# Banded attention with queries and keys in two orders, and one unit of scores per head

## What is computed

```python
OFFSETS = sorted(set(range(0, 33)) | {48, 64, 96, 128, 192, 64, 96, 128, 192, 256, 384})
scores = stack([einsum('bhnd,bhnd->bhn', q, shift(k, delta)) for delta in OFFSETS]) * scale
scores = scores + pos_bias.T[None, :, None, :]          # 16 heads of 16 columns
scores = where(n < delta, -inf, scores)
alpha = softmax(scores, axis=-1)
out = sum over i of alpha[..., i:i+1] * shift(v, OFFSETS[i])
return flat(out) * sigmoid(x @ Wgate + bgate) @ Wout + bout
```

## Time and profile before

| | us |
|---|---|
| median of 3 runs | 3774.55 |
| the profiled execution, its own time | 3782.0 |
| its span, first to last instruction | 3780.3 |
| PE busy in the span | 3176.4 (84%) |
| DVE busy | 1747.6 (46%) |
| ACT busy | 1189.4 (31%) |
| POOL busy | 352.9 (9%) |

### The profile page before, as it was taken

How to read it: one execution, slowest core, us unless ns; L and a number is a source line. 1 busy time by engine, 2 the same in 40 slices (tenths; PEclk the granted TensorE clock), 3 DMA queues, 4 the chain that set the end, 5 groups by cost and what they waited for, 6 DMA issues and landing times. The chain is left out here.

```text
span 3780.3 us, 99336 instructions
## 1 busy us (share of the span) xinstructions
PE 3176.4 (84%) x44860; PEld 1864.3 (49%) x44860; DVE 1747.6 (46%) x3244; ACT 1189.4 (31%) x1486; POOL 352.9 (9%) x334
## 2 busy tenths in 40 slices
PE   1688888888788888879957899999999898997898
PEld 0456565656565666634443444444444444443345
DVE  5334333434333333361074665666666656664302
ACT  0122222222222222232002545554545554553300
POOL 0000000000000000000002111121212121100000
PEclk9788888888788888789957999999999999998896
DMA  5422222222222222126813222222222222312394
GB/s 131 109 68 74 68 74 68 74 71 71 71 71 68 74 68 74 33 92 266 359 15 84 52 52 60 56 56 52 52 53 59 52 60 52 68 19 93 124 419 175
DMA packets 235041, 343.30 MB, mean 91 GB/s; under 512 B 115962, under 2 KB 144452, under 8 KB 218244
## 3 DMA queue, kind: packets, MB, share of 16 engines
q1 hardware_dynamic: 222452, 334.40, 30.9%
q10 hardware_dynamic: 12176, 2.66, 0.5%
HBM read 266.15 MB, written 69.24 MB: 89 GB/s over the span
## 5 line engine op out<-in xcount | busy, mean ns | idle before, releaser
L1351 DVE TENSOR_REDUCE b_tops<-b_slot 128x8 f32<-128x1024 f32 x576 | 680.4, 1220 | 361.5 <-PE b_slot L1208 182.6
L1388 ACT ACTIVATE b_probs<-b_slot 128x1024 f32<-128x1024 f32 x576 | 583.1, 1023 | 551.2 <-PE b_slot L1208 395.5
L711 DVE TENSOR_TENSOR a_probs<-a_scores,a_bias_k 128x512 f32<-128x512 f32 x256 | 176.6, 690 | 554.5 <-PE a_scores L570 318.3
L803 ACT ACTIVATE a_probs<-a_probs 128x512 f32<-128x512 f32 x256 | 161.5, 631 | 589.7 <-DVE a_probs L711 588.6
L1228 PE MATMUL b_outT_ps<-b_probs,b_v 128*17 128x128 f32 (+3 forms) x4608 | 318.0, 384 | 6.2 <-ACT b_probs L1388 5.5
L1208 PE MATMUL b_slot<-b_q_stack,b_k_stack 99*128 99x512 bf16 (+3 forms) x1280 | 275.8, 322 | 43.3 <-DVE b_tops L1351 32.8
L1208 PE MATMUL b_slot<-b_k_stack,b_q_stack 96*128 96x512 bf16 (+3 forms) x1280 | 267.1, 323 | 29.4 <-DVE b_tops L1351 20.6
L1155 POOL TENSOR_SCALAR_AFFINE_SELECT b_probs<-b_probs 128x1024 f32<-128x1024 f32 x128 | 139.8, 1093 | 809.5 <-ACT b_probs L1388 809.5
L1208 PEld LDWEIGHTS b_slot<-b_q_stack,b_k_stack 99*128 99x128 bf16 x1280 | 107.2, 100 | 204.6 <-DVE b_tops L1351 61.9
L1208 PEld LDWEIGHTS b_slot<-b_k_stack,b_q_stack 96*128 96x128 bf16 x1280 | 97.6, 98 | 185.4 <-DVE b_tops L1351 61.6
L1762 PE MATMUL f_ps<-f_w_ring,f_hidT 128*32 128x256 f32 x1024 | 184.0, 381 | 2.1 <-ACT f_hidT L1803 2.1
(11 more groups left out here) (215 smaller groups left out, 4492.1 us busy)
## 6 DMA issues: line engine op xcount, KB each, us to landing
f_w_ring<-in_L_ffn_w_dram SPq DMA_DIRECT2D x128, 1024.0 KB, 10.1
parts_dram<-a_parts SPq DMA_DIRECT2D x96, 256.0 KB
parts_dram<-b_parts SPq DMA_DIRECT2D x96, 256.0 KB
a_k_stack<-parts_dram SPq DMA_DIRECT2D x128, 128.0 KB, 3.0
b_k_stack<-parts_dram SPq DMA_DIRECT2D x64, 256.0 KB, 7.1
a_q_stack<-parts_dram SPq DMA_DIRECT2D x64, 192.0 KB, 3.0
b_q_stack<-parts_dram SPq DMA_DIRECT2D x32, 384.0 KB, 4.6
values_dram<-a_v_stage SPq DMA_DIRECT2D x32, 272.0 KB, 2.6
```

The source lines that it names most:

```text
L711: dve.tensor_tensor(dst[:, :].rearrange("p (t c) -> p t c", c=64), src[:, :].rearrange("p (t c) -> p t c", c=64), bias_k[k][:, HG * g + h, ...
L803: act.activation(dst[:, :], dst[:, :], ACT.Exp).then_inc(probs_ready, 1)
L1351: ins = dve.tensor_reduce(out, src, AX.X, ALU.max)
L1388: act.activation(probs_of(b, g, u, h)[:, :], slot_of(step)[:, :], ACT.Exp).then_inc(taken_act, 1)
```

## The change

- **Two orders.** `parts` holds each part twice, as it is and sorted by residue; the far products read the second copy without a stride (`products`, one function for near and far now). The new step `turn` makes the copies on POOL, three strided copies of 1,024 elements. Spills are three DMAs of 512 KB, a pair's stacks seven DMAs of 1,536 KB in all.
- **Room.** Instead of two sets of stacks of four heads there is a ring of three for two heads each (`ring`). `parts`, `v_near`, `v_far`, `v_stage` and the probabilities have one buffer; the f32 projection `full`, the normalised tokens and `flatT` are one tile.
- **Projections.** q or k is made in one piece of 1,024 columns: DVE adds its bias, ACT rounds `part0`, POOL subtracts (`rest1`), ACT rounds `part1`, POOL subtracts (`part2`) and turns. `part0` waits on ACT until the spill before has landed. They stand in groups 1 (q and k of the first half, both behind the far products) and 3 (q between the scores, k behind the far products).
- **Units.** A unit is one head, near and far together, 128 x 1024: four a group. PSUM is three slots of two banks that scores, maxima and all else share in turn. The next group's maxima of head h follow the scores of head h.
- **Maxima's rows.** `mt` is 16 matmuls into two places (one for each order), taken by DVE and ACT; `mrow` is four DMAs. Both stand ahead of the group's own far products, which now follow its near ones.

The core of the diff:

```diff
-            for step in (which, "part1", "part2"):
-                out += [(step, b, half, c) if step == which else (step, b, half, c, which) for c in range(2)]
-            out.append(("spill", b, half, which))
+            out += [(which, b, half)] + [(step, b, half, which) for step in ("part0", "rest1", "part1", "part2", "turn", "spill")]
...
+            tops = [[("mx",) + after + (h,)] if more else [] for h in range(HG)]
...
+            cuts = [len(first) * k // 3 for k in range(4)]
+            seq += [("vin", b, g), ("S", b, g, 0)] + tops[0] + [("S", b, g, 1)] + operands(n + 3) + tops[1]
+            seq += first[cuts[0]:cuts[1]] + [("S", b, g, 2)] + tops[2] + first[cuts[1]:cuts[2]] + [("S", b, g, 3)] + operands(n + 4)
+            seq += tops[3] + ([("fparts",) + after] if more else []) + first[cuts[2]:cuts[3]] + near[0:4]
+            seq += ([("fp",) + after, ("mred",) + after] if more else []) + near[4:8]
+            seq += ([("mt",) + after, ("mrow",) + after] if more else []) + far
+            seq += last + [("ote", b, g)]
...
+            if g in (1, 3):
+                p = projections(b + 1, g // 2)
+                last = p + last if g == 1 else last
+                first = first + p[0:7] if g == 3 else first
+                last = p[7:] if g == 3 else last
...
+def ring(b, g, pair):
+    return (2 * (b * G + g) + pair) % 3
...
-        parts = [sb(f"parts{m}", [P, PARTS, N], BF16) for m in range(2)]
-        q_stack = [sb(f"q_stack{n}", [ALL_ROWS, HG, N], BF16) for n in range(2)]
-        k_stack = [sb(f"k_stack{n}", [ALL_ROWS, HG, N], BF16) for n in range(2)]
...
+        parts = sb("parts", [P, PARTS, 2, N], BF16)
+        q_stack = [sb(f"q_stack{n}", [ALL_ROWS, 2, 2, N], BF16) for n in range(3)]
+        k_stack = [sb(f"k_stack{n}", [ALL_ROWS, 2, 2, N], BF16) for n in range(3)]
...
+        full = zb[:, :, :].rearrange("p i d -> p (i d)")
...
+        slots = [ctx.enter_context(nc.psum_tensor(f"a_slot{n}", [P, N], F32)) for n in range(3)]
...
-        scores_ps = [ctx.enter_context(nc.psum_tensor(f"a_scores{n}", [P, 512], F32)) for n in range(NS)]
...
-        aux_ps = [ctx.enter_context(nc.psum_tensor(f"a_aux{n}", [P, 512], F32)) for n in range(NA)]
...
+                    elif kind == "rest1":
+                        _, b, half, which = step
+                        pool.wait_ge(part0_done, count("part0", "part0", b, half, which))
+                        pool.tensor_tensor(full, full, parts[:, 0, 0, :], ALU.subtract).then_inc(rest1_done, 1)
+                    elif kind == "part2":
+                        _, b, half, which = step
+                        pool.wait_ge(part1_done, count("part1", "part1", b, half, which))
+                        pool.tensor_tensor(parts[:, 2, 0, :], full, parts[:, 1, 0, :], ALU.subtract).then_inc(part2_done, 1)
+                    elif kind == "turn":
+                        _, b, half, which = step
+                        pool.wait_ge(part2_done, count("part2", "part2", b, half, which))
+                        for part in range(PARTS):
+                            pool.tensor_copy(parts[:, part, 1, :].rearrange("p (r a) -> p r a", r=LINKS),
+                                             parts[:, part, 0, :].rearrange("p (a r) -> p r a", r=LINKS)).then_inc(turned, 1)
...
-                        sp.wait_ge(part2_done, count("part2", "part2", b, half, 1, which))
+                        sp.wait_ge(turned, PARTS * count("turn", "turn", b, half, which))
...
-                            sp.dma_start(scratch["parts"].ap()[m, half, :, part], parts[m][:, part, :]).then_inc(spilled[m], 16)
+                            sp.dma_start(scratch["orders"].ap()[m, half, :, part], parts[:, part, :, :]).then_inc(spilled, 16)
...
+                        sp.wait_ge(spilled, SPILL * count("spill", "spill", b, g // 2, "k"))
+                        if 2 * (b * G + g) + pair >= 3:
+                            b0, g0, pair0 = pair_of(2 * (b * G + g) + pair - 3)
+                            sp.wait_ge(filled, count("filled", "S", b0, g0, 2 * pair0 + 1))
...
+                        for h in range(HG):
+                            sp.dma_start(q_stack[ring(b, g, h // 2)][QK_ROWS:ALL_ROWS, h % 2, :, :], neg_rows[PARTS * h:PARTS * (h + 1), :, :]
+                                         ).then_inc(mrows_in, 16)
...
-                            ins = pe.matmul(dst[RES * r2:RES * (r2 + 1), 64 * pair:64 * (pair + 1)],
-                                            left[rows, h, r:N:LINKS], right[rows, h, r:N:LINKS],
...
+                        ins = pe.matmul(dst[RES * r2:RES * (r2 + 1), at:at + 64], left[rows, h, 1, RES * r:RES * (r + 1)],
+                                        right[rows, h, 1, RES * r:RES * (r + 1)], start=start, stop=True, skip_group_check=True)
...
+                        for at, i in [(at, i) for at in (AT_ROWS, 2 * AT_ROWS) for i in range(NT)]:
+                            ins = pe.matmul(dst[at:at + HG * PARTS, i * P:(i + 1) * P], neg_parts[:, :, :, i].rearrange("p h a -> p (h a)"),
+                                            ident16[:, :], start=True, stop=True, skip_group_check=True)
...
+                        if c == 0 and k == 0:
+                            pe.wait_ge(probs_ready, count("S", "S", b, g, HG - 1))
...
+                    elif kind == "part0":
+                        _, b, half, which = step
+                        act.wait_ge(taken_dve, count("taken_dve", which, b, half))
+                        hold(act, spilled, SPILL * (count("part0", *step) - 1))
+                        act.activation(parts[:, 0, 0, :], full, ACT.Copy).then_inc(part0_done, 1)
```

More of the change, by code:

```diff
@@ L223, in others @@
-        if g == 3 and b < B - 1:
-            v = values(b + 1)
-            for u in range(4):
-                out[u] += v[2 * u:2 * u + 2]
-            out[5].append(("vin", b + 1, 0))
-        return out
-    seq = tokens(0) + projections(0, 0)
-    for g in range(2):
-        seq += operands(0, g, 0) + operands(0, g, 1)
-    seq += values(0) + [("vin", 0, 0)]
-    for steps in maxima(0, 0):
-        seq += steps
-    left = []
+            first = [("ot", b - 1, 3), ("gmul", b - 1), ("at", b - 1, 0), ("op", b - 1, 0), ("at", b - 1, 1), ("op", b - 1, 1)] if b else []
```

619 lines of the change are left out of this document (283 added, 336 removed).

## The result

The changed kernel takes 4551.65 us (median of 4 runs, 4545.16 to 4559.0) against 3775.85 for the kernel before in the same job: a ratio of 1.2057, 95% interval 1.2035 to 1.2079. It is slower, as forecast, but by 776 us instead of 255, far above the range of 3860 to 4130. The profiled execution took 4559.0, its span is 4557.0.

The account below looks back on a forecast made before the run. PE bounds the kernel before; the new chain ahead of the stacks outweighs PE's savings: 217.4 us a sequence against 186.2, with prologue +64, gives +229, clock +30, so 3782.0 becomes 4041, called 4030; range 3860 to 4130.

Parts of the forecast that it names:

- The rule weighed: POOL's turning copies: a read step over 8 bytes costs 2.9, not 1.9 cycles; three copies 7.2 us, not 4.8; kernel 4110.
- a sequence, step by step: Banded stage: PE's work and waits through groups 1, 2, 3 and 0 sum to 217.4 us a sequence, against 186.2.
- chain, q filled to maxima of head 2: q's rounding, turn and spill, then k's, then `vin` and the pair's stacks landing, before group 2's head 2 maxima: 51.1 us.
- the rest of group 2: After the chain: maxima 1.5, v 6.1, head 3 and exponential 3.1, products 8.8, v again 6.1: 25.7 us.
- group 3, to head 2's maxima in group 0: q filled at 10.4 us, k at 33.5, `part0` at 38, SP free at 52.4, head 2's maxima at 64.6 us.
- the rest of group 0: Maxima, transposes, output products, head 3, products with v and gates one after another: 40.0 us, with handovers 40.5.
- The clock: PE restarts at the low clock after long waits: +30 us over the kernel, between 0 and 60.
- The prologue: Before the first scores: both halves' q and k chains in turn, first scores at 204.5 us instead of 140.5, +64.
- Slow copies: Rival, POOL's strided copies half as dear again: 9.6 us a sequence, +77, kernel 4107 us; chance 0.15.
- Far product without gain: Rival, stride does not hold the far product: some +12 us a sequence, kernel 4125 us; chance 0.06.
- Better cover: Rival, chain and PE cover each other better: 8 us less a chain, kernel 3910 us; chance 0.13.
- The short chain: Rival, POOL and spills at a third of the prices, PE sets the end: 158.9 us a sequence, kernel 3595; chance 0.08.

Follow-up runs that it names:

- when spread: Ring-of-four, one-order kernel with projections, gates and v products moved among the group's far products with v: 3892.51 us, ratio 1.0315 to the kernel before.
- the version with one order: Changed kernel's steps with one order, a ring of four stacks, two buffers for parts, outputs ahead of projections: 3922.93 us, 1.0403 to the kernel before.
- the later spill: Changed kernel with k's spill put behind the next pair's stack requests on SP, nothing else changed: 4213.54 us, ratio 1.1129 to the kernel before.

## Where the prediction held and where it failed

**The direction and its reason held.** The far product got faster and could not pay, since the stacks come late. PE stands twice a sequence before L570 until a stack's DMA has landed, for 27 to 31 us; L805 waits for the spill; and q's own chain is 14.0 us to the end of the turn (1183.8 to 1197.8). That last figure was right by luck, for two prices were wrong and cancelled: POOL's subtractions take 2.12 us, not 2.7 (four times L490 counts what is fixed in an instruction four times), and a copy 2.0, not 1.6.

**The rule weighed.** A copy's median is 2,032 ns, its mean 2,183:

```profile
L458 POOL COPY a_parts<-a_parts x96: 2005/2032/4122, 110.3 to 2205.2; 128x1024 bf16<-128x1024 bf16 x96
```

My row said 1.6. Beside the subtractions of this trace it is dearer still: in the earlier trace rows a cast takes 398 ns where a subtraction takes 670, six tenths, so with a subtraction at 2.12 a copy of packed memory would be 1.26, and 2.03 is 1.6 times that. If what is fixed in an instruction is taken off first (0.19 us, from 0.67 for 256 elements and 2.12 for 1,024), the packed copy would be 1.03 and the factor 2.0. Both are estimates; no run tried the copy without a step. The Trainium skill ("GPSIMD Engine Reference", "Performance pitfalls for Q7 kernels") has 2.9 to 1.9 cycles for it, 1.5 times: the trace agrees with the direction, and its estimates lie a little above that factor. I had weighed the rule against L482 and let the row win; its repeated elements hid the step.

**What failed is the size of three terms and one that was left out** (the second below), in "a sequence, step by step" and in the chain. From the group 1 that starts at 1137.55 us to the next sequence's at 1421.71 there are 284.2 us where I had 217.4:

| stretch | predicted | measured |
|---|---|---|
| group 1 and q | 35.5 | 46.3 |
| chain, q filled to maxima of head 2 | 51.1 | 62.1 |
| the rest of group 2 | 25.7 | 36.3 |
| group 3, to head 2's maxima in group 0 | 64.6 | 88.3 |
| the rest of group 0 | 40.5 | 51.1 |

1. *The chain, +11.* q's part and k's part (1209.98 to 1222.6) were right. The spill landed 12.2 us after its issue, not 10.4; and SP was slow: k's spill 4.0 us instead of 1.8, `vin` 7.5 instead of 3.3, the stacks landed 8.0 after their last issue instead of 5.8. I had taken issue times from quiet rows; the trace of before has slower ones, `vin` right behind a spill at 716.18 with 3.44 us where my row has 2.09.
2. *PE's instructions, not in the sum.* The rest of group 2 is 10.6 longer, and 8.5 of that are issue waits in its products with v (1.64, 5.19, 1.70). I priced these products at 8.8 us by the earlier trace rows; with the issue waits and the low clock they took 18.1. The rest of group 0, 10.6 longer as well, has 6.2 us of them (1.01, 1.39, 1.85, 1.99), and its gates took 14.8 us instead of 12.2, half of them at the low clock. Over the kernel issue waits at L606 and L616 are 201 us, where before had 31. Those at L606 come with the bytes (77 against 17, shown), most of those at L616 with packing all products with v behind one another (124 against 46 when spread, shown on the version with one order).
3. *Bytes in every group.* A pair's stack, asked for behind head 1's scores at 1140.4, let PE go on at 1150.28: 9.9 us, not 6.2. Group 1 has that, 3.3 us of issue waits and 6.1 (2.62, 3.52) for the normalised tokens; group 3 has 7.6 of issue waits (4.13, 1.34, 2.15) ahead of k, and a slower SP behind it (4.0 for the spill, 7.4 for `vin`). So k's slot was filled 48.0 us into group 3, where I had 33.5, and its `part0` (1331.68) waited for DVE's bias and not for q's spill: there the chain was set by PE coming late, not by the landing that I had counted.
4. *The clock, a little past its bounds.* The stage's 0.70 has the standing time in it; PE's own work tells more. Before it was busy 1245; 183 less for the far products (316 against 133.5), 26 more for `mt` (34.1 against 8.6) and some 10 less for 16 matmuls of q and k that now run before the first scores would be some 1079, and it is 1151: some 70 us, where I had 30 between 0 and 60. That all of it is the clock is argued, not shown.

The prologue was 27 us longer too (first scores 231.4, I said 204.5): q's first slot was filled at 102.4 instead of 94, and the spill of the second half's q, which stood behind the stacks of three pairs, was issued at 165.8 and landed at 186.3, 20 us instead of 10.4.

The step that failed is therefore the one that took each price from a quiet row, a spill alone and a pair's stacks alone, and gave PE's small matmuls no wait for issue. Such rows could not show what doubling the bytes does to what shares the DMA engines and SP's queue (352 us, by bytes alone), nor what packing the products with v does to PE. The range of 3860 to 4130 took each unknown one at a time, when several of them had the bytes as their cause and moved together.

**The rivals.** Slow copies: partly so, but 14.0 us came out the same. Far product without gain: no, 0.37 us from start to start at the high clock (1187.53 to 1187.90) and 0.57 at the low one (1302.65 to 1303.22), against 1.18; I said 0.35. Better cover: no, the chain was 11 us longer where this rival had it 8 shorter. The short chain: 4059 without any chain.

## What to carry to other kernels

When a change doubles the bytes of a transfer, take again every price that touches the queue: landing, the issue on its engine, and the waits of an engine that runs many small instructions; a quiet row is the lower bound of each. Before a long-latency step is put in a queue, ask which requests stand behind it that do not need it: one such step moved here was 338 us, without a byte less. And a wait counts only if nothing else ends just behind it: taking away the outputs' wait (129 to 134 us) was worth nothing, on its own and behind the later spill, taking away the rows' (76 us) was worth nothing, and the smallest (57 us) won 87.

## What the runs showed of the hardware

**A request takes longer to issue right behind a spill on the same queue.** The four requests of `vin` took 1.79 us at 1407.08, 3.11 at 1283.92 and 6.26 right behind a spill (1226.63, shown above); the four of `mrow` 2.92 and 5.53:

```profile
1283.92 3.11 SPq L514 DMA_DIRECT2D a_v_near<-values_dram  x4
1273.44 2.92 SPq L496 DMA_DIRECT2D a_q_stack<-a_row_home  x4
1316.82 4.02 SPq L475 DMA_DIRECT2D orders_dram<-a_parts  x3
1320.95 5.53 SPq L496 DMA_DIRECT2D a_q_stack<-a_row_home  x4
```

It goes with the bytes of the spill ahead: three requests of 512 KB took 4.0 us and `vin` behind them 6.2; with 256 KB each, in the kernel before and with one order, a spill by itself took 2.0 and `vin` behind it 2.3 to 3.8 (3.44 at 716.18 of the kernel before, 3.71 at 858.83 with one order). It does not go with how busy the DMA engines are: their share was 0.73 during the 3.11 us and 0.59 during the 6.26. What holds the queue was not tried.

**Bulk loads lengthen PE's waits for issue.** The page lists a DMA kind "instruction" beside the data's, and the wait of 4.13 us below follows a stack's requests. PE, then SP, in the same 12 us:

```profile
q8 instruction: 354, 5.80, 0.6%
```

```profile
1309.30 0.29 PE L606 MATMUL a_outT_ps<-a_probs,a_v_near 128*17 128x64 f32 x3
1313.71 3.50 PE L606 MATMUL a_outT_ps<-a_probs,a_v_near 128*17 128x64 f32 x125 [4.13 <-issue]
```

```profile
1303.38 1.25 SPq L488 DMA_DIRECT2D a_q_stack<-orders_dram  x3
1304.99 1.71 SPq L488 DMA_DIRECT2D a_k_stack<-orders_dram  x4
```

The two kernels that differ by bytes alone show that the bytes lengthen these waits (77 against 17 us at the near products with v). That PE waits for instructions which the loads hold up is the likely reading and was not measured. Where the DMA engines are nearly idle (a share of 0.07 from 1401.6 to 1404.6) the far products with v still pause for 1.3 to 2.3 us after about every 128 matmuls, which with a weight load each are 256 instructions: a matmul takes some 12 ns there, less, it seems, than its instructions take to arrive. This is read from the gaps and from what spreading did (124 to 46 us), not measured by itself.
